# Expert weights of sparse blocks, brought to their buffers by two DMAs of the SyncE queue instead of by GpSimd

## The chip, the core and the metric

The kernel runs on one core of one Trainium2 chip. The metric is the time of one execution on the device in microseconds (us): 1469.63, the median of 3 runs (1466.67 to 1473.55). Engines are named as in the profile: PE is TensorE, PEld its weight load, ACT is ScalarE, DVE is VectorE, POOL is GpSimd, SP is SyncE. SP issues most of the DMAs here; a name with a q (SPq) is the engine's sequencer.

## The reference

Eight sequences of 512 tokens, 128 features wide, pass through five layers with residual sums:

```python
x = x + 0.5 * _L0_ffn_ref(_layernorm(x), ...)      # 8 experts, two per token   (first 8-expert stage)
x = x + _L0_attn_ref(_layernorm(x), ...)
x = x + 0.5 * _L0_ffn_ref(_layernorm(x), ...)      # the same weights again    (second 8-expert stage)
x = x + 0.5 * _L1_ffn_ref(_layernorm(x), ...)      # 16 experts
x = x + _L1_attn_ref(_layernorm(x), ...)           # a scan
x = x + 0.5 * _L1_ffn_ref(_layernorm(x), ...)
```

In an 8-expert layer a router picks two of eight experts for each token, and each expert is `gelu(x @ w1 + b1) @ w2 + b2` with a hidden width of 512:

```python
probs = jax.nn.softmax(xf @ w_router, axis=-1)
topk_w, topk_idx = jax.lax.top_k(probs, 2)
h = jax.nn.gelu(jnp.einsum('te,ieh->tih', xf, w1) + b1)
out = jnp.einsum('tih,ihe->tie', h, w2) + b2
out = jnp.sum(out * weights[..., None], axis=1)
```

## The kernel before

The change lies in the two 8-expert stages, both written by `moe0_phase` (the variable `occ` is 0 in the first and 1 in the second). A stage does not compute every expert for every token. Sequence 0 is computed densely: 8 blocks of 512 tokens, one for each expert. The tokens of the other seven sequences are sorted by expert: GpSimd writes their normalised rows to a DRAM table `xs_rows` by indirect DMAs, each expert padded to blocks of 512 rows, which makes `NBLK` = 21 sparse blocks. Which expert a block belongs to is known only at run time and stands in a small table in SBUF, `expert_t`. So a stage walks over 29 blocks: `i` = 0 to 7 dense (`D` = 8), and `i` = D + j for the sparse blocks j = 0 to 20.

All eight experts' weights lie in SBUF in `w_all`, split into a high and a low part, 4 x 512 columns for an expert: 1024 for the up product and 1024 for the down product. A dense block reads its expert's columns there, since they are fixed when the program is built. A sparse block reads copies, in `w_up[j % 2]` and `w_down[j % 2]`: two buffers each, of 128 x 1024 elements (512 KB). Before the change GpSimd makes these copies, in `take_up` (L1237) and `take_down` (L1242): it loads the expert's number into a register (L1284) and casts from a source column that the register gives (L1240, L1245). Each copy counts on the semaphore `w_taken`.

PE works a block in four chunks `c`. For each chunk it does three matmuls of the up product (`up0`, L908; matmuls at L904, L905, L906) and then three of the down product of the chunk that lies 6 chunks back (`down0`, L924). So in the step of block D + t it does up(t, 0), down(t-2, 2), up(t, 1), down(t-2, 3), up(t, 2), down(t-1, 0), four transposes back of block t-3 (`back_pe`, L974), up(t, 3), down(t-1, 1). At the start of the step stand the four transposes of the rows of the next block (`xT_pe`, L843). ACT applies gelu (L945) and makes half of the rounded copies (L950); DVE makes the other half (L958), the remainders (L960, L856) and the copy out (L990).

A buffer comes free when PE is done with it: `w_up[j % 2]` with the last up product of block j-2, at the end of the step of that block; `w_down[j % 2]` with the last down product of block j-2, which is the sixth group of the step of block j, in the middle of that step (after 12 of its 24 matmuls). `up0` and `down0` wait for `w_taken` in front of their first chunk.

The order of SP's queue in the sparse blocks is written out in `sync`: it loads block rows into three buffers `xb` (L1335, 256 KB each, up to seven ahead, held back by the wait for the transposes of the block three before), stores the result rows of each block to `ys_rows` (L1349, 256 KB, after a wait for DVE's copy), and in the first stage, behind the stores of blocks 3 to 10, saves one expert's split weights to DRAM (`keep0`, L754, 1 MB each), which the second stage reads back (L761). Every wait in this queue holds what stands behind it.

Of the kernel before, what the change touches and what calls it, by code (L numbers as in the profile page):

```python
# [7 lines left out]
F32 = mybir.dt.float32  # L8
# [9 lines left out]
NE0, HID = 8, 512  # L18
HC = HID // P
# [16 lines left out]
NBLK = (2 * (B - 1) * T + NE0 * (T - 1)) // T  # L36
# [24 lines left out]
def build(nc, a, out, phases=PHASES):  # L61
    nc.disable_value_cache = True
    with ExitStack() as ctx:
# [98 lines left out]
        w_staged = [sem(f"w_staged{i}") for i in range(4)]  # L162
# [195 lines left out]
        def load_weights(q):  # L358
# [16 lines left out]
            for dst, src in weights:  # L375
# [2 lines left out]

        moe0_sems, moe1_sems = {}, {}
        moe0_names = ("pe_step", "act_step", "dve_step", "pool_step", "dve_chain", "w_hi", "w_lo", "w_kept", "sent0", "sent1", "pads",  # L380
                      "x_ld0", "x_ld1", "x_ld2", "xT_ps", "up_ready", "act_done", "dve_done", "down_done", "yback", "w_taken")
        moe0_sems.update({k: sem(f"moe0_{k}") for k in moe0_names})
        rs_ = moe0_sems

# [294 lines left out]
        def moe0_phase(n):  # L679
# [75 lines left out]

            def reload0(e):
                if e > 3:
                    nc.sync.wait_ge(w_staged[e % 4], 32 * 3)
# [144 lines left out]
            def hi_lo(out_bank, w_hi, w_lo, x_hi, x_lo, start, stop):  # L903
                nc.tensor.matmul(out_bank, w_hi, x_hi, start=start, stop=False)  # L904
                nc.tensor.matmul(out_bank, w_hi, x_lo, start=False, stop=False)  # L905
                return nc.tensor.matmul(out_bank, w_lo, x_hi, start=False, stop=stop)  # L906

            def up0(i, c):  # L908
                u = HC * i + c
                if c == 0:  # L910
                    nc.tensor.wait_ge(s["dve_done"], dve_no("xl", prep(i)))
                    if dense(i) and occ:
                        nc.tensor.wait_ge(w_staged[i % 4], 32 * (3 + i // 4))
                    elif dense(i):
                        nc.tensor.wait_ge(s["w_lo"], i + 1)
                    else:
                        nc.tensor.wait_ge(s["w_taken"], 2 * NBLK * occ + max(1, 2 * (i - D)))
                if u > 3:
                    nc.tensor.wait_ge(s["act_done"], act_no("gelu", (u - 4) // HC, c))
                w = w_all[:, i * 4 * HID:i * 4 * HID + 2 * HID] if dense(i) else w_up[(i - D) % 2]  # L920
                q = prep(i) % 2
                hi_lo(bank[u % 4][:], w[:, c * P:(c + 1) * P], w[:, HID + c * P:HID + (c + 1) * P], xh[q][:], xl[q][:], True, True).then_inc(s["up_ready"], 1)

            def down0(i, c):  # L924
                u = HC * i + c
# [316 lines left out]
            def take_down(g, j, ex_):  # L1242
                if j > 1:
                    g.wait_ge(s["down_done"], U0 + HC * (D + j - 1))
                nc.gpsimd.tensor_copy(w_down[j % 2], w_all[:, bass.ds(ex_ * (4 * HID) + 2 * HID, 2 * HID)]).then_inc(s["w_taken"], 1)  # L1245

            def routed(g, what):

# [15 lines left out]
            def gpsimd(g):  # L1264
                after_phases(g, n)
                f = base(n + 1)
                if occ == 0:
                    route_consts(g)
                    for b in ORDER[0]:
                        seq_root(g, occ, b)  # L1270
                    group_send(g, occ, 0, pace=lambda k, m: routed(g, {4: "l4", 8: "l5", 12: "l6", 14: "l7"}.get(k)))
                    group_send(g, occ, 1, pace=lambda k, m: after_start(g, k))
                    group_send(g, occ, 2, pace=lambda k, m: beside(g, 16 + k * 15 // 16, 0))
                else:
                    seq_root(g, occ, B - 1)
# [4 lines left out]
                g.wait_ge(s["x_ld0"], 16 * (per_ld[0] * occ + 1))  # L1280
                ex_ = nc.gpsimd.value_load(expert_t[0:1, 0:1], min_val=0, max_val=NE0 - 1)
                take_up(g, 0, ex_)
                for j in range(NBLK):
                    e1 = nc.gpsimd.value_load(expert_t[0:1, j + 1:j + 2], min_val=0, max_val=NE0 - 1) if j + 1 < NBLK else None  # L1284
                    if j + 1 < NBLK:
                        take_up(g, j + 1, e1)
                    take_down(g, j, ex_)
                    ex_ = e1
                    if D + j == NORM - 3 and occ == 0:
                        g.wait_ge(w_loaded, 16 * N_WEIGHTS)  # L1290
                        for w, w_p in ((wq, wq_p), (wl, wl_p)):
                            last = g.tensor_copy(w_p[:].rearrange("p (d h) -> p d h", d=HD), w[:].rearrange("p (h d) -> p d h", d=HD))
                        last.then_inc(tables_ready, 1)
                    if D + j == NORM - 2:
                        norm_b(f)
                    for b, tile in GATHERS.get(j, ()):
                        stored_by(g, occ, b)
                        gather(g, occ, b, (tile, tile + 1))
                if occ == 0:
                    early_parts["pool"](g)  # L1300

            def sync(q_):
# [16 lines left out]
                    load_weights(q_)  # L1319
                if occ:  # L1320
                    for k in range(4):
                        q_.wait_ge(w_staged[k], 32 * 4)
# [14 lines left out]
                x_load(0)  # L1337
                q_.wait_ge(s["x_ld0"], 16 * (per_ld[0] * occ + 1))
                for i in range(1, 7):
                    x_load(i)  # L1340
                for i in range(NBLK):
                    if i + 7 < NBLK:
                        x_load(i + 7)
                    if occ == 0 and i == NBLK - 3:
                        early_parts["saves"]()
                    if occ == 0 and i == NBLK - 2:
                        early_parts["loads"]()
                    q_.wait_ge(s["dve_done"], dve_no("y", D + i))
                    q_.dma_start(rows(ys_rows, i), yb[i % 2]).then_inc(y_stored[i % 2], 16)  # L1349
                    if occ == 0 and 2 < i < 3 + NE0:  # L1350
                        keep0(i - 3)

            return {"tensor": tensor, "scalar": scalar, "vector": vector, "gpsimd": gpsimd, "sync": sync, "zeros": zeros}


# [397 lines left out]
        def attn_phase(n):  # L1753
# [195 lines left out]
            def early_act(i, c):  # L1949
                if (i, c) == (ALL - 2, 3):  # L1950
                    biased_act("q", 0, 6)
                if (i, c) == (ALL - 1, 1):
                    biased_act("k", 0, 6)
                    nc.scalar.wait_ge(moe0_sems["w_taken"], 2 * NBLK * (occ0 + 1))
                    part1_act("k", 0)

            def early_dve(v):
                v.wait_ge(moe0_sems["w_taken"], 2 * NBLK * (occ0 + 1))
                split_dve(v, "k", 0)

            def early_v_dve(v):
                v_dve(v, 0, bank[6])

            def early_pool(g):
                g.wait_ge(moe0_sems["w_taken"], 2 * NBLK * (occ0 + 1))
                split_pool(g, "q", 0)

            def early_saves():
# [1147 lines left out]
```

## Time and profile before

| | |
|---|---|
| time, median of 3 runs | 1469.63 us (1466.67 to 1473.55) |
| span of the profiled execution, first to last instruction | 1464.5 us |
| what lies around the span, by the median | 5.1 us |
| PE, DVE, ACT, POOL busy | 1277.9, 1149.4, 887.0, 520.0 us |
| sparse blocks of the first 8-expert stage | about 113 to 273 us |
| sparse blocks of the second | about 792 to 949 us |

The profiled execution has no time of its own beside its span; 1464.5 lies 2.2 us under the shortest of the three runs. In the rows below, a row of a timeline has its start, its duration, engine, line and operation, the tile written and the tiles read, and in square brackets how long the engine had sat idle before it and what released it. Buffers cut from the shared region all have the name `shared`. Lines are those of the kernel before.

### The profile page before, as it was taken

Reading aid. Unit: us, or ns where it says so; the run is one execution under the profiler, and the core shown is the slowest. Engines: PE = TensorE matmul, PEld = TensorE weight load, DVE = VectorE, ACT = ScalarE, POOL = GpSimd, SP = SyncE. Lnnn points to the kernel's source line nnn. Section 1 sums busy time; section 2 is a strip of 40 time slices with the busy share of each in tenths; the row PEclk is TensorE's granted clock in tenths of the full one; section 3 lists DMA queues with packets and bytes.
Section 4 is the critical chain, followed back from the end, with each engine's and each line's share of the span. In section 5 each row is a group of like instructions: output and inputs, shape, how many; then the busy total and the mean of one; then the engine's idle time right before and its main releaser. Section 6 shows DMA issues by size and latency. Waiting matters only on the chain.

```text
span 1464.5 us, 20418 instructions
## 1 busy us (share of the span) xinstructions
PE 1277.9 (87%) x6496; PEld 766.6 (52%) x6496; DVE 1149.4 (78%) x2430; ACT 887.0 (61%) x1402; POOL 520.0 (36%) x757
## 2 busy tenths in 40 slices
PE   6768999779999889998679999899999889899998
PEld 5557777412222222222267777666666345566665
DVE  6857879789889989889466989878886664877875
ACT  6846767348788768887577667633333477334432
POOL 6773427444534424511273335514430120210100
PEclk9989999779999989999889999999999999999999
DMA  8521453332212202210151122255453011054434
GB/s 285 143 86 52 151 196 117 129 90 86 86 45 88 86 24 91 92 35 2 66 224 56 58 73 86 78 126 114 105 118 73 13 32 24 1 127 107 92 84 116
DMA packets 88679, 133.94 MB, mean 91 GB/s; under 512 B 16756, under 2 KB 42836, under 8 KB 87548
## 3 DMA queue, kind: packets, MB, share of 16 engines
q1 hardware_dynamic: 81404, 117.93, 28.5%
q0 software_dynamic: 7168, 14.69, 3.4%
q8 instruction: 53, 0.87, 0.3%
q14 instruction: 54, 0.44, 0.1%
HBM read 82.23 MB, written 47.45 MB: 89 GB/s over the span
## 4 chain that ended last, share of the span: by engine, by line
PE 55%; DVE 25%; issue 8%; ACT 7%; DMA 3%; POOL 1%; SPq 1%; DVEq 0%; ACTq 0%; POOLq 0%
DVE shared L2170 6%; PE bank L1557 6%; PE pair L904 5%; PE pair L906 5%; PE pair L905 5%; PE bank L2248 5%; PE pair L1469 3%; PE pair L1471 3%; PE pair L1470 3%; PE pair L2230 3%; PE pair L2162 3%; DVE shared L960 3%; ACT shared L2238 2%; DVE shared L1545 1%; PE bank L974 1%
## 5 line engine op out<-in xcount | busy, mean ns | idle before, releaser
L2170 DVE TENSOR_REDUCE shared<-pair 128x2 f32<-128x1024 f32 x256 | 309.7, 1217 | 41.6 <-PE pair L2162 38.7
L2238 ACT ACTIVATE shared<-pair 128x1024 f32<-128x1024 f32 x256 | 260.5, 1022 | 51.7 <-PE pair L2230 50.2
L960 DVE TENSOR_TENSOR shared<-shared 128x512 fp32r<-128x512 f32 x232 | 193.2, 842 | 76.9 <-ACT shared L950 73.4
L904 PE MATMUL pair<-shared 128*128 128x512 f32 x464 | 198.2, 427 | 9.9 <-DMA shared<-w_keep 3.9
L1524 ACT ACTIVATE shared<-pair 128x512 f32<-128x512 f32 x144 | 85.6, 596 | 179.5 <-PE pair L1471 179.3
L906 PE MATMUL pair<-shared 128*128 128x512 f32 x464 | 187.3, 404 | 0.0
L905 PE MATMUL pair<-shared 128*128 128x512 f32 x464 | 187.3, 404 | 0.0
L945 ACT ACTIVATE shared<-pair,shared 128x512 f32<-128x512 f32 x168 | 115.9, 690 | 72.7 <-PE pair L906 67.3
L1469 PE MATMUL pair<-shared 128*128 128x512 f32 x288 | 154.4, 536 | 4.9 <-DVE shared L1479 4.9
L2248 PE MATMUL bank<-shared 128*9 128x512 f32 x1024 | 139.6, 618 | 4.5 <-ACT shared L2238 4.3
L277 POOL DMA_INDIRECT staged<-ys_rows,slots x112 | 117.7, 1051 | 58.4 <-ACT shared L2238 32.1
L645 POOL DMA_INDIRECT xs_rows<-shared,slots x112 | 118.3, 1057 | 55.5 <-issue 26.8
L1536 DVE TENSOR_TENSOR shared<-shared,pair 128x512 f32<-128x512 f32 x128 | 87.0, 682 | 58.2 <-ACT shared L1524 56.9
L1557 PE MATMUL bank<-shared,down_w 128*128 128x512 f32 x256 | 129.1, 595 | 0.8 <-DVE shared L1545 0.8
L2162 PE MATMUL pair<-shared 48*128 48x512 bf16 x512 | 104.1, 405 | 21.3 <-ACT shared L2238 10.6
L1471 PE MATMUL pair<-shared 128*128 128x512 f32 x288 | 115.5, 401 | 0.0
L1470 PE MATMUL pair<-shared 128*128 128x512 f32 x288 | 114.9, 399 | 0.0
L2230 PE MATMUL pair<-shared 51*128 51x512 bf16 x512 | 102.3, 397 | 5.9 <-DVE shared L2170 5.2
L904 PEld LDWEIGHTS pair<-shared 128*128 128x128 f32 x464 | 91.1, 196 | 28.2 <-issue 8.0
L2230 PEld LDWEIGHTS pair<-shared 51*128 51x128 bf16 x512 | 24.7, 93 | 150.9 <-issue 87.8
L906 PEld LDWEIGHTS pair<-shared 128*128 128x128 f32 x464 | 90.3, 195 | 21.5
L905 PEld LDWEIGHTS pair<-shared 128*128 128x128 f32 x464 | 90.9, 196 | 16.9 <-issue 0.2
(380 smaller groups left out, 2262.7 us busy)
## 6 DMA issues: line engine op xcount, KB each, us to landing
shared<-p_coef_rows SPq DMA_DIRECT2D x64, 512.0 KB, 6.0
shared<-xs_rows SPq DMA_DIRECT2D x42, 256.0 KB, 2.8
ys_rows<-shared SPq DMA_DIRECT2D x42, 256.0 KB, 2.0
w_keep<-shared SPq DMA_DIRECT2D x8, 1024.0 KB, 4.8
shared<-w_keep SPq DMA_DIRECT2D x16, 512.0 KB, 9.6
shared<-p_q_parts SPq DMA_DIRECT2D x64, 96.0 KB, 2.4
shared<-p_k_parts SPq DMA_DIRECT2D x64, 96.0 KB, 2.5
xs_rows<-shared SPq DMA_DIRECT2D x1, 5376.0 KB, 18.4
```

The source lines that it names most:

```text
L904: nc.tensor.matmul(out_bank, w_hi, x_hi, start=start, stop=False)
L905: nc.tensor.matmul(out_bank, w_hi, x_lo, start=False, stop=False)
L906: return nc.tensor.matmul(out_bank, w_lo, x_hi, start=False, stop=stop)
L960: nc.vector.tensor_tensor(hl[u % RING][:], hid[u % RING][:], hh[u % RING][:], ALU.subtract).then_inc(s["dve_done"], 1)
L1469: nc.tensor.matmul(out_bank, w_hi, x_hi, start=start, stop=False)
L1470: nc.tensor.matmul(out_bank, w_hi, x_lo, start=False, stop=False)
L1471: return nc.tensor.matmul(out_bank, w_lo, x_hi, start=False, stop=stop)
L1557: nc.tensor.matmul(bank[6][:], w, h, start=(j == 0), stop=(j == IT - 1)).then_inc(s["down_done"], 1)
L2170: nc.vector.tensor_reduce(mneg[:, i, 2 * c:2 * c + 2], pair_of("max", b, m)[:], AX_X, ALU.max, negate=True).then_inc(s["mx_read"], 1)
L2230: last = nc.tensor.matmul(pair_of("exp", b, 2 * st + p)[:, f, :], ka[par][rows, c, kt * P:(kt + 1) * P], qa[par][rows, c, :], start=True, ...
L2238: nc.scalar.activation(probs[st % 2][:, 2 * p:2 * p + 2, :], pair_of("exp", b, 2 * st + p)[:], ACT.Exp, scale=scale).then_inc(s["exp_done" ...
L2248: last = nc.tensor.matmul(bank[6][32 * hh:32 * hh + HD + 1, :], v_all[:, b * TILES + kt, hh % 2 * (H // 2) + g * HG // 2 + hh // 2, :], pr ...
```

## The change

GpSimd no longer copies expert weights. `take_up` and `take_down` become one DMA each, issued by SP, with a source column from a register that SP loads; the two buffers of each kind count on the four semaphores `w_staged`, which `up0` and `down0` now wait for. SP's queue is written anew: in the turn `t` of its loop stand the load of the next expert's number, the down weights of block t, the up weights of block t + 1, the rows of block t + 3, the store of block t - 4, and in the first stage a save. The wait for the first rows in front of the second load is gone. Three users of `w_all`'s space after the first stage wait for the four semaphores (`weights_taken`) instead of `w_taken`.

```diff
-                        nc.tensor.wait_ge(s["w_taken"], 2 * NBLK * occ + max(1, 2 * (i - D)))
+                        nc.tensor.wait_ge(w_staged[(i - D) % 2], taken_by(i - D))
...
-                        nc.tensor.wait_ge(s["w_taken"], 2 * NBLK * occ + min(2 * (i - D) + 3, 2 * NBLK))
+                        nc.tensor.wait_ge(w_staged[2 + (i - D) % 2], taken_by(i - D))
...
-            def take_up(g, j, ex_):
+            def take_up(q_, j, at):
                 if j > 1:
-                    g.wait_ge(s["up_ready"], U0 + HC * (D + j - 1))
-                nc.gpsimd.tensor_copy(w_up[j % 2], w_all[:, bass.ds(ex_ * (4 * HID), 2 * HID)]).then_inc(s["w_taken"], 1)
+                    q_.wait_ge(s["up_ready"], U0 + HC * (D + j - 1))
+                q_.dma_start(w_up[j % 2].bitcast(F32), w_all[:, bass.ds(at * (4 * HID), 2 * HID)].bitcast(F32)).then_inc(w_staged[j % 2], 16)
...
                 for j in range(NBLK):
-                    e1 = nc.gpsimd.value_load(expert_t[0:1, j + 1:j + 2], min_val=0, max_val=NE0 - 1) if j + 1 < NBLK else None
-                    if j + 1 < NBLK:
-                        take_up(g, j + 1, e1)
-                    take_down(g, j, ex_)
-                    ex_ = e1
+                    g.wait_ge(s["up_ready"], U0 + HC * (D + j))
...
                 x_load(0)
-                q_.wait_ge(s["x_ld0"], 16 * (per_ld[0] * occ + 1))
-                for i in range(1, 7):
-                    x_load(i)
-                for i in range(NBLK):
-                    if i + 7 < NBLK:
-                        x_load(i + 7)
...
+                of = {0: expert(0)}
+                take_up(q_, 0, of[0])
+                x_load(1)
+                x_load(2)
+                for t in range(NBLK + 4):
+                    if t + 1 < NBLK:
+                        of[t + 1] = expert(t + 1)
+                        if t == 0:
+                            take_up(q_, 1, of[1])
+                    if t < NBLK:
+                        take_down(q_, t, of.pop(t))
+                    if 0 < t and t + 1 < NBLK:
+                        take_up(q_, t + 1, of[t + 1])
+                    if t + 3 < NBLK:
+                        x_load(t + 3)
+                    if t > 3:
+                        store(t - 4)
...
+            def weights_taken(eng):
+                for k in range(4):
+                    eng.wait_ge(w_staged[k], (64 + 16 * per_st[k % 2]) * (occ0 + 1))
...
                     biased_act("k", 0, 6)
-                    nc.scalar.wait_ge(moe0_sems["w_taken"], 2 * NBLK * (occ0 + 1))
+                    weights_taken(nc.scalar)
                     part1_act("k", 0)
```

On SP, before, one turn in the middle of the first stage's sparse blocks is a load of rows, a store and a save (here two turns):

```order
L1335 DMA shared<-xs_rows 128x512 [waits moe0_xT_ps]
L1349 DMA ys_rows<-shared 128x512 [waits moe0_dve_done]
L754 DMA w_keep<-shared 128x2048
L1335 DMA shared<-xs_rows 128x512 [waits moe0_xT_ps]
L1349 DMA ys_rows<-shared 128x512 [waits moe0_dve_done]
L754 DMA w_keep<-shared 128x2048
```

On SP now, one turn at the same place; with their numbers the buffers are `shared12` = `w_all`, `shared20` and `shared21` = `w_down`, `shared3` and `shared4` = `w_up`; L1334 loads the expert's number, L1248 and L1243 are the two copies:

```order
L1334 TENSOR_LOAD shared13
L1334 ISA x2
L1248 ISA [waits moe0_down_done]
L1248 DMA shared21<-shared12 128x1024
L1243 ISA [waits moe0_up_ready]
L1243 DMA shared3<-shared12 128x1024
```

The copy of the up weights (L1243) stands behind the copy of the down weights (L1248) and behind its wait for `down_done`; behind them follow the load of rows, the store and the save as before.

On POOL, before, at the same place:

```order
L1284 TENSOR_LOAD shared
L1284 ISA x2
L1240 ISA [waits moe0_up_ready]
L1240 COPY shared<-shared 128x1024
L1245 ISA [waits moe0_down_done]
L1245 COPY shared<-shared 128x1024
```

There the copy of the up weights of block j + 1 stood ahead of that of the down weights of block j, with a wait of its own. On POOL now nothing of this is left: behind the indirect sends of the dense blocks stand at once the small copies, the norm and the gathers:

```order
L645 DMA xs_rows<-shared,slots 10752x128 [waits moe0_up_ready] x15
L1288 COPY wq_p<-w_q 128x128 [waits moe0_up_ready,w_loaded]
L1288 COPY wl_p<-w_l 128x128
L187 TENSOR_SCALAR var<-mv 128x4 [waits moe0_up_ready,mv_ready]
L189 TENSOR_TENSOR rs_y<-var,neg_half 128x4 [waits var_ready]
L277 DMA staged<-ys_rows,slots 128x128 [waits moe0_up_ready,y_stored0,y_stored1]
```

On PE, before, at the start of the step of a sparse block (the name `pair` is a pair of PSUM banks):

```order
L843 MATMUL bank<-ident,shared 128x128 [waits moe0_dve_done,moe0_x_ld0]
L843 MATMUL bank<-ident,shared 128x128 x3
L904 MATMUL pair<-shared 128x512 [waits moe0_act_done,moe0_w_taken,moe0_dve_done]
L905 MATMUL pair<-shared 128x512
L906 MATMUL pair<-shared 128x512
```

There the first up matmul waits for GpSimd's count. On PE now, the same place:

```order
L843 MATMUL bank<-ident,shared 128x128 [waits moe0_dve_done,moe0_x_ld0]
L843 MATMUL bank<-ident,shared 128x128 x3
L904 MATMUL pair<-shared 128x512 [waits moe0_act_done,w_staged0,moe0_dve_done]
L905 MATMUL pair<-shared 128x512
L906 MATMUL pair<-shared 128x512
```

No matmul has moved; the wait is now for a DMA's semaphore. The waiting L904 stands behind the transposes of the next block's rows and ahead of everything else of its step.

## Rows read from the trace of the kernel before

**Rows 1.** Timeline, PE, first stage: starts of steps 2 and 3, first matmul of step 20.

```profile
127.12 0.60 PE L843 MATMUL bank<-ident,shared 128*128 128x128 f32 x4
133.55 0.60 PE L843 MATMUL bank<-ident,shared 128*128 128x128 f32 x4
...
260.18 0.40 PE L904 MATMUL pair<-shared 128*128 128x512 f32 x1
```

**Rows 2.** Windows of 18 steps in each stage: busy us (instructions) by engine.

```profile
core 0: us, PE busy (x) PEld busy (x) DVE busy (x) ACT busy (x) POOL busy (x), PEclk, DMA share, GB/s
127.47:260.18 132.71, 122.39 (x591) 98.32 (x590) 115.27 (x184) 89.63 (x147) 59.32 (x56) 0.97 0.40 133
804.82:934.57 129.75, 119.86 (x587) 96.77 (x586) 117.28 (x198) 89.39 (x146) 57.91 (x54) 0.99 0.22 72
```

**Rows 3.** Timeline: one step of block 4 of the first stage.

```profile
143.01 0.42 DVE L958 CAST shared<-shared 128x512 fp32r<-128x512 f32 x1
...
143.65 0.47 PE L904 MATMUL pair<-shared 128*128 128x512 f32 x1
...
146.28 0.39 PE L906 MATMUL pair<-shared 128*128 128x512 f32 x1
...
146.85 1.04 POOL L1245 CAST shared<-shared 128x1024 fp32r x1 [2.52 <-PE pair L906]
...
148.64 0.69 DVE L960 TENSOR_TENSOR shared<-shared 128x512 fp32r<-128x512 f32 x1 [0.20 <-ACT shared L950]
...
149.37 1.20 POOL L1240 CAST shared<-shared 128x1024 fp32r x1 [1.47 <-PE pair L906]
...
149.70 1.41 DVE L960 TENSOR_TENSOR shared<-shared 128x512 fp32r<-128x512 f32 x1
...
150.08 0.48 PE L904 MATMUL pair<-shared 128*128 128x512 f32 x1
```

**Rows 4.** Groups by line, 113.5 to 245 us: count, busy us, mean ns.

```profile
L960 DVE TENSOR_TENSOR shared<-shared 128x512 fp32r<-128x512 f32 x72 | 66.7, 930 | 17.3 <-ACT shared L950 15.8
...
L958 DVE CAST shared<-shared 128x512 fp32r<-128x512 f32 x36 | 18.4, 511 | 0.0
```

**Rows 5.** The same, 790 to 945 us.

```profile
L960 DVE TENSOR_TENSOR shared<-shared 128x512 fp32r<-128x512 f32 x88 | 75.0, 862 | 14.6 <-ACT shared L950 13.0
...
L958 DVE CAST shared<-shared 128x512 fp32r<-128x512 f32 x42 | 24.0, 571 | 0.4 <-ACT shared L945 0.3
```

**Rows 6.** Timeline, PE: idle times in the next-to-last sparse step of each stage.

```profile
255.82 2.04 PE L1812 MATMUL bank<-xnT,wq_p 128*128 128x512 f32 x2 [3.28 <-issue]
...
932.72 0.63 PE L974 MATMUL bank<-ident,shared 128*128 128x128 f32 x4 [2.73 <-DVE shared L990]
```

**Rows 7.** DMA issues of the page: KB each, median us from issue to landing.

```profile
ys_rows<-shared SPq DMA_DIRECT2D x42, 256.0 KB, 2.0
w_keep<-shared SPq DMA_DIRECT2D x8, 1024.0 KB, 4.8
...
shared<-shared SPq DMA_DIRECT2D x72, 32.0 KB, 2.0
```

**Rows 8.** Short windows with DMA traffic (columns of rows 2).

```profile
740.00:745.00 5.00, 5.00 (x17) 3.95 (x16) 1.82 (x3) 3.27 (x7) 3.78 (x5) 0.66 1.03 418
166.80:167.30 0.50, 0.50 (x4) 0.37 (x3) 0.50 (x1) 0.50 (x2) 0.40 (x1) 1.00 1.21 459
169.30:169.80 0.50, 0.50 (x5) 0.46 (x4) 0.47 (x3) 0.15 (x1) 0.50 (x1) 1.00 1.21 262
```

**Rows 9.** Timeline: the first sparse block, and the end of the first stage.

```profile
109.95 1.11 PE L843 MATMUL bank<-ident,shared 128*128 128x128 f32 x4 [9.62 <-DMA shared<-xs_rows]
110.89 2.03 POOL L1240 CAST shared<-shared 128x1024 fp32r x2 [4.68 <-DMA shared<-xs_rows]
...
264.16 1.04 POOL L1245 CAST shared<-shared 128x1024 fp32r x1 [9.42 <-PE pair L906]
...
265.76 0.68 ACT L945 ACTIVATE shared<-pair,shared 128x512 f32<-128x512 f32 x1
```

More of the change, by code:

```diff
@@ L380, in build @@
         moe0_names = ("pe_step", "act_step", "dve_step", "pool_step", "dve_chain", "w_hi", "w_lo", "w_kept", "sent0", "sent1", "pads",
-                      "x_ld0", "x_ld1", "x_ld2", "xT_ps", "up_ready", "act_done", "dve_done", "down_done", "yback", "w_taken")
+                      "x_ld0", "x_ld1", "x_ld2", "xT_ps", "up_ready", "act_done", "dve_done", "down_done", "yback")
         moe0_sems.update({k: sem(f"moe0_{k}") for k in moe0_names})
@@ L757, in reload0 @@
                 if e > 3:
-                    nc.sync.wait_ge(w_staged[e % 4], 32 * 3)
+                    nc.sync.wait_ge(w_staged[e % 4], 32 * 3 + 16 * per_st[e % 2])
                 for k in range(2):
@@ L906, in hi_lo, with taken_by @@
                 return nc.tensor.matmul(out_bank, w_lo, x_hi, start=False, stop=stop)
+            def taken_by(j):
+                return 64 * (occ + 1) + 16 * (per_st[j % 2] * occ + j // 2 + 1)
             def up0(i, c):
@@ L912, in up0 @@
                     if dense(i) and occ:
-                        nc.tensor.wait_ge(w_staged[i % 4], 32 * (3 + i // 4))
+                        nc.tensor.wait_ge(w_staged[i % 4], 32 * (3 + i // 4) + 16 * per_st[i % 2])
                     elif dense(i):
@@ L1235, in vector, with take_down @@
                     combine(v, occ, 2)
-            def take_up(g, j, ex_):
+            def take_up(q_, j, at):
                 if j > 1:
-                    g.wait_ge(s["up_ready"], U0 + HC * (D + j - 1))
-                nc.gpsimd.tensor_copy(w_up[j % 2], w_all[:, bass.ds(ex_ * (4 * HID), 2 * HID)]).then_inc(s["w_taken"], 1)
-            def take_down(g, j, ex_):
+                    q_.wait_ge(s["up_ready"], U0 + HC * (D + j - 1))
+                q_.dma_start(w_up[j % 2].bitcast(F32), w_all[:, bass.ds(at * (4 * HID), 2 * HID)].bitcast(F32)).then_inc(w_staged[j % 2], 16)
+            def take_down(q_, j, at):
                 if j > 1:
-                    g.wait_ge(s["down_done"], U0 + HC * (D + j - 1))
-                nc.gpsimd.tensor_copy(w_down[j % 2], w_all[:, bass.ds(ex_ * (4 * HID) + 2 * HID, 2 * HID)]).then_inc(s["w_taken"], 1)
+                    q_.wait_ge(s["down_done"], U0 + HC * (D + j - 1))
+                q_.dma_start(w_down[j % 2].bitcast(F32), w_all[:, bass.ds(at * (4 * HID) + 2 * HID, 2 * HID)].bitcast(F32)).then_inc(w_staged[2 + j % 2], 16)
             def routed(g, what):
@@ L1279, in gpsimd @@
                     group_send(g, occ, 3, pace=lambda k, m: beside(g, (28 + k) * 7 // 9, 2))
-                g.wait_ge(s["x_ld0"], 16 * (per_ld[0] * occ + 1))
-                ex_ = nc.gpsimd.value_load(expert_t[0:1, 0:1], min_val=0, max_val=NE0 - 1)
-                take_up(g, 0, ex_)
                 for j in range(NBLK):
-                    e1 = nc.gpsimd.value_load(expert_t[0:1, j + 1:j + 2], min_val=0, max_val=NE0 - 1) if j + 1 < NBLK else None
-                    if j + 1 < NBLK:
-                        take_up(g, j + 1, e1)
-                    take_down(g, j, ex_)
-                    ex_ = e1
+                    g.wait_ge(s["up_ready"], U0 + HC * (D + j))
                     if D + j == NORM - 3 and occ == 0:
@@ L1321, in sync @@
                     for k in range(4):
-                        q_.wait_ge(w_staged[k], 32 * 4)
+                        q_.wait_ge(w_staged[k], 32 * 4 + 16 * per_st[k % 2])
                 else:
@@ L1335, in x_load, with expert, store @@
                     q_.dma_start(xb[i % 3], rows(xs_rows, i)).then_inc(s[f"x_ld{i % 3}"], 16)
-                x_load(0)
-                q_.wait_ge(s["x_ld0"], 16 * (per_ld[0] * occ + 1))
-                for i in range(1, 7):
-                    x_load(i)
-                for i in range(NBLK):
-                    if i + 7 < NBLK:
-                        x_load(i + 7)
+                def expert(j):
+                    return nc.sync.value_load(expert_t[0:1, j:j + 1], min_val=0, max_val=NE0 - 1)
+                def store(i):
                     if occ == 0 and i == NBLK - 3:
@@ L1351, in sync @@
                         keep0(i - 3)
+                x_load(0)
+                of = {0: expert(0)}
[15 more added lines that the diff above has]
+                        store(t - 4)
             return {"tensor": tensor, "scalar": scalar, "vector": vector, "gpsimd": gpsimd, "sync": sync, "zeros": zeros}
@@ L1953, in early_act @@
                     biased_act("k", 0, 6)
-                    nc.scalar.wait_ge(moe0_sems["w_taken"], 2 * NBLK * (occ0 + 1))
+                    weights_taken(nc.scalar)
                     part1_act("k", 0)
             def early_dve(v):
-                v.wait_ge(moe0_sems["w_taken"], 2 * NBLK * (occ0 + 1))
+                weights_taken(v)
                 split_dve(v, "k", 0)
@@ L1964, in early_pool @@
             def early_pool(g):
-                g.wait_ge(moe0_sems["w_taken"], 2 * NBLK * (occ0 + 1))
+                weights_taken(g)
                 split_pool(g, "q", 0)
```

## The prediction

> **What bounds the kernel now.** I read the page's busy times first, then windows over the two 8-expert stages, then the timeline of single steps of PE, DVE, POOL and SP, and last the DMA issues. In the sparse blocks the step is set by PE where nothing else happens: its starts lie 6.43 us apart (127.12 to 133.55) [rows 1]. From the first up matmul of block 2 to that of block 20 the 18 steps took 132.71 us in the first stage and 129.75 in the second [rows 2], 262.5 together or 7.29 a step. At 6.43 each, 36 steps would be 231.5 us, so 31.0 us are steps that something stretched. DVE is the suspect: it was busy 6.46 us a step (115.27 and 117.28 over 36) [rows 2], and PE's long idle times end at DVE's copy or on what follows it (2.73 and 3.28 us) [rows 6]. The reader should see in one step [rows 3] that DVE's remainder L960 takes 0.69 us alone and 1.41 when it overlaps POOL's copy of 149.37. The means over each stage, 930 and 862 ns for L960 and 511 and 571 for L958 [rows 4, 5], are all above the 0.69 and 0.42 of an undisturbed one [rows 3], so the copies cost DVE 72 x 0.24 + 88 x 0.17 + 36 x 0.09 + 42 x 0.15 = 41.8 us in both stages. POOL's own time matters to nobody else here.
>
> **What is removed.** 84 casts (21 blocks, two copies, two stages) of about 1.0 to 1.2 us leave POOL. On the path this is worth what DVE loses by them: 41.8 us of DVE time, 1.16 a step, leaving 5.3 a step. Against a step of 6.43 DVE then has room, and most of the 31.0 us should go. A burst of DVE work longer than the room of one step still shows, so I leave 1 us in each stage.
>
> **What is added on PE's path.** A copy by POOL was ready soon after its buffer came free: the up copy starts at the end of a step (149.37) and the next step's matmul at 150.08 does not need it, since it serves the block behind that. Now the up copy of block t + 1 stands in SP's queue behind the wait for the down products of block t - 2, which end in the middle of step t. It is needed at the first up matmul of step t + 1. This makes a loop from step to step: twelve matmuls, then the two DMAs, then the twelve matmuls of the next step, with the other twelve and the eight transposes beside the DMAs.
> - The twelve matmuls: from 143.65 to 146.28 + 0.39, 3.02 us [rows 3].
> - Waking the queue and PE: POOL began 0.18 us after that end [rows 3]; I take 0.2 for SP's wake, its register instruction and PE's start.
> - X, from the issue of the down copy to the landing of the up copy, 2 x 512 KB through one queue. No row shows a large copy from SBUF to SBUF. From below: a store of 256 KB lands in 2.0 us [rows 7], and 0.79 MB more at the fastest stretch, 459 GB/s [rows 8], add 1.7: X = 3.7. From above: a 1 MB save lands in 4.8 [rows 7], behind a store. The nearest in kind are the small copies from SBUF to SBUF, 2.0 us for 32 KB [rows 7], in which the bytes are almost nothing; with 1.05 MB at the 418 GB/s of the reload [rows 8], 2.5 us, that is 4.4 to 4.5. I take X = 4.3, nearer to that row than to the store.
>
> The loop is 3.02 + 0.2 + 4.3 = 7.52 us, over PE's 6.43 and DVE's 5.3, so it sets the step: PE waits about 1.1 us at the start of each. 36 x 7.52 = 270.7, with 2 us left over from DVE 272.7, against 262.5: **+10.2 us**. X enters 36 times; the break-even is X = 4.02.
>
> The trace gives the two copies no price as one DMA. The Trainium skill, in "DMA: Bandwidth & Descriptors", section "Anatomy of one DMA", fits 2.0 us plus the bytes at 436 GB/s; for 1.05 MB as one transfer that is an estimate of 4.4, and the sum by it would be +13.8. It is fitted there to DMAs that GpSimd issues. The same page's rules for authors say to issue a DMA early and to wait late; here the issue is late by half a step, and that is the rule that speaks against the change.
>
> **The other edits.** SP's load of the expert number has no row of its own; on POOL landing, load and start of the copy lay within 0.94 us (109.95 to 110.89) [rows 9]. On SP it runs while the queue would wait for the middle of the next step: five issues of 0.3 to 0.5 us and this load are about 3 of 7.5 us, so it costs nothing. Uncovered it would add its 0.9 to each loop. The loads of rows and the stores stand behind the copies and are wanted one and a half steps later: nothing. In eight steps of the first stage a 1 MB save stands last in the turn. 2.62 MB a turn at 418 GB/s is 6.3 us, but where the save fell to 262 GB/s [rows 8] it is 7.8, which would hold the next copies 0.3 us: I take 1 us in all, bounds 0 and 5. At the start of each stage the second load of rows no longer waits for the first (it stands behind the first copy instead); I take -0.5, bounds -2 and +1. At the end of the first stage ACT waits for all copies before it goes on to gelu (265.76); the last down copy started on POOL at 264.16 and took 1.04 [rows 9]. By DMA, 512 KB by the same reckoning takes 3.0, so ACT is about 2 us late, and PE with it: +2, bounds 0 and +3. Against that PE was slow (2.04 us for the pair of matmuls at 255.82) after its idle time [rows 6]; without the idle time I take -1.5, bounds -3 and 0. These make +1.0.
>
> **Sum.** +11 us on the span of 1464.5, that is 1475.5; with the 5.1 us by which the median lies above the span, **1480.6**.
>
> **Rivals.**
> - *The copies are quick enough, and DVE's relief wins* (faster). In the same loop X is 3.7 or less: the step is 6.9, 36 steps are 249.1 us, with 2 left over 251.1 against 262.5, and with the +1.0 of the other edits the change is -10.4: 1459. For it: the store's row, and PE's excess of 31.0 us. Against it: the 2.0 us of a copy with hardly any bytes. It decides from X below 3.8.
> - *The two effects cancel.* X near 4.0: the lost half step equals the removed stalls, within 7 us of 1470. For it: X = 4.02 lies between the two rows.
> - *The copy is slow*, because each DMA engine reads and writes SBUF at once and goes at 262 GB/s, as in the save: X = 1.9 + 4.0 = 5.9, the step 9.1, +69 with the other edits: 1538. For it only that one stretch; a DMA that both reads and writes SBUF in bulk has no row.
> - *PE's clock drops* because it idles in each step. At 3.28 us of idle time the next matmuls were slow [rows 6], but the windows with all stalls have 0.97 and 0.99 [rows 2]; a tenth of the clock over PE's 242 busy us there is 24 us. I count it within the slow side.
>
> **How the numbers follow.** About 0.5 % (7 us) is what a measurement of this kernel can tell from no change. Forecast, X from 4.2 to 5.0 (+8 to +36): 0.45. Slow copy or clock: 0.08. Cancelling (X 3.8 to 4.2): 0.26. Quick copies: 0.21. So slower 0.53, same 0.26, faster 0.21. The range leaves out most of the slow copy, and the quickest of the quick: 1459 to 1508; the forecast's own range is 1477 to 1506.
>
> **What would show it.** In the changed profile the first up matmul of most sparse steps should wait for a DMA from `shared` to `shared`, about 1 us, some 36 times; steps should be even, near 7.5 us; L960 should fall to about 0.69 and POOL by some 90 us; the long idle times before L974 should be gone. Steps at 6.4 to 6.9 without that wait would make the forecast wrong towards faster; L960 still at 0.86 or more would mean that POOL's copies were not what stretched it.

## The result, and the profile after

The changed kernel takes 1496.2 us (median of 4 runs, 1492.4 to 1502.8) against 1471.6 us for the kernel before in the same comparison (4 runs, 1466.7 to 1474.8). The ratio is 1.0191 with a 95 % interval of 1.0148 to 1.0235: slower by 25 us between the medians and by 28 us by the ratio, more than the 7 us that can be told from no change. Back matmuls are now at L977, the remainder at L963, the cast at L961, gelu at L948; L1248 and L1243 are the copies of the down and the up weights, L1331 the load of rows, L1342 the store.

The page of the changed kernel, span and busy times:

```profile
span 1497.6 us, 20444 instructions
## 1 busy us (share of the span) xinstructions
PE 1284.1 (86%) x6496; PEld 769.1 (51%) x6496; DVE 1102.7 (74%) x2430; ACT 887.1 (59%) x1402; POOL 424.9 (28%) x673
```

POOL lost 95 us and DVE 47 us, as a relief of POOL should show, and the span still grew by 33.1 us over the 1464.5 before. That is 8.5 us more than the medians differ: the profiled execution before was a quick one, and this one (1499.3 us) lies 3 us above its median. What lies around the span is here 1.7 us, so most of the 5.1 us named for the kernel before is such spread. The windows over the same 18 steps of each stage as in [rows 2], with the same columns:

```profile
128.50:274.71 146.21, 122.39 (x591) 96.68 (x589) 95.72 (x187) 90.40 (x148) 18.99 (x20) 1.00 0.69 252
817.64:961.00 143.36, 121.37 (x588) 96.23 (x586) 97.67 (x201) 89.60 (x146) 18.08 (x18) 1.00 0.56 198
```

The 36 steps took 289.57 us (8.04 each) against 262.46: +27.1 of the +33.1. PE was busy 243.76 us, 1.5 more than before, and its clock is not lower, so the new time is PE's waiting. DVE's busy time fell from 232.55 to 193.39 us. The groups by line, 113.5 to 262 us and then 803 to 973 us, answer to [rows 4, 5]:

```profile
L963 DVE TENSOR_TENSOR shared<-shared 128x512 fp32r<-128x512 f32 x73 | 50.7, 696 | 53.7 <-ACT shared L953 52.5
L961 DVE CAST shared<-shared 128x512 fp32r<-128x512 f32 x36 | 15.5, 429 | 0.0
...
L963 DVE TENSOR_TENSOR shared<-shared 128x512 fp32r<-128x512 f32 x88 | 60.6, 692 | 51.5 <-ACT shared L953 50.1
L961 DVE CAST shared<-shared 128x512 fp32r<-128x512 f32 x42 | 17.6, 420 | 0.1
```

So the copies by POOL had stretched DVE: the remainder's mean of 930 and 862 ns became 696 and 692. What replaced that is seen on PE, in the timeline of two steps of the first stage:

```profile
152.12 0.47 PE L904 MATMUL pair<-shared 128*128 128x512 f32 x1 [1.23 <-DVE shared L961]
...
154.75 0.40 PE L906 MATMUL pair<-shared 128*128 128x512 f32 x1
...
158.19 0.60 PE L843 MATMUL bank<-ident,shared 128*128 128x128 f32 x4
160.06 0.47 PE L904 MATMUL pair<-shared 128*128 128x512 f32 x1 [1.27 <-DVE shared L961]
...
168.02 0.47 PE L904 MATMUL pair<-shared 128*128 128x512 f32 x1 [1.29 <-DVE shared L963]
```

In most steps PE now idles 1.2 to 1.3 us before its first up matmul, and steps lie 7.94 us apart where nothing else happens. The rows name DVE as the releaser, but the step's time is accounted for by the two copies, and the experiments on them move it. SP's queue in the same step:

```profile
155.28 0.50 SPq L1248 DMA_DIRECT2D shared<-shared  x1
155.92 0.50 SPq L1243 DMA_DIRECT2D shared<-shared  x1
156.47 0.78 SPq L1331 DMA_DIRECT2D shared<-xs_rows  x1
157.29 1.20 SPq L1342 DMA_DIRECT2D ys_rows<-shared  x1
```

All landings of L1243 in that execution:

```profile
DMA to landing us min/median/max: 2.9/4.0/5.6
```

With the median landing, 155.92 + 4.0 = 159.92, and PE starts at 160.06. From the issue of the down copy to the landing of the up copy is 0.64 + 4.0 = 4.64 us: this is X. The loop is 3.03 us of twelve matmuls (152.12 to 155.15), 0.13 to the issue, 4.64, and 0.14 to PE's start: 7.94. (Twelve matmuls are four groups of three: the last down product of block t - 2 is the fourth group of a step, not the sixth as the description of the kernel has it.)

The rest of the +33.1 lies outside these steps. In stage 1, step 2 began 1.0 us later. From step 20 of stage 1 to its last back matmuls but one it took 19.1 us (274.71 to 293.83) against 15.6 before (260.18 to 275.77). PE at the beginning of that stretch, and then ACT in it:

```profile
274.71 0.47 PE L904 MATMUL pair<-shared 128*128 128x512 f32 x1 [2.32 <-DVE shared L993]
275.80 0.63 PE L904 MATMUL pair<-shared 128*128 128x512 f32 x1
278.00 1.05 PE L904 MATMUL pair<-shared 128*128 128x512 f32 x1
```

```profile
280.65 0.69 ACT L1888 ACTIVATE shared<-bank,vecs 128x512 f32<-128x512 f32 x1
283.46 0.62 ACT L1893 CAST shared<-shared 128x512 bf16<-128x512 f32 x1 [2.13 <-issue]
283.99 0.68 ACT L948 ACTIVATE shared<-pair,shared 128x512 f32<-128x512 f32 x1
```

The granted clock was 0.59 from 274.7 to 277.0 us and 0.75 to 280.0, behind PE's 2.32 us of idle time. ACT idles 2.13 us where its code waits for the last copies' semaphores, with a gelu that PE needs behind it. Between the stages and behind the second one the two executions differ by -5.2 and +6.7 us, nearly all of it in code that the change does not touch.

### The profile page after: what moved, and what is told of

It reads as the page before. It is cut to its first block, busy times and chain, and to the rows that moved or that the text cites. A ratio compares the mean times of both kernels' runs of the same rounds, so it can differ in the third digit from the quotient of the medians.

```text
span 1497.6 us, 20444 instructions
## 1 busy us (share of the span) xinstructions
PE 1284.1 (86%) x6496; PEld 769.1 (51%) x6496; DVE 1102.7 (74%) x2430; ACT 887.1 (59%) x1402; POOL 424.9 (28%) x673
## 4 chain that ended last, share of the span: by engine, by line
PE 52%; DVE 26%; issue 9%; ACT 7%; DMA 3%; POOL 1%; SPq 1%; DVEq 0%; ACTq 0%; POOLq 0%
PE bank L1569 6%; DVE shared L2186 6%; PE pair L904 5%; PE pair L906 4%; PE bank L2264 4%; PE pair L905 4%; DVE shared L963 4%; PE pair L1481 3%; PE pair L1483 3%; PE pair L1482 3%; PE pair L2246 3%; PE pair L2178 3%; ACT shared L2254 2%; ACT shared L953 2%; DVE shared L961 1%
## 5 line engine op out<-in xcount | busy, mean ns | idle before, releaser
L963 DVE TENSOR_TENSOR shared<-shared 128x512 fp32r<-128x512 f32 x232 | 160.5, 697 | 156.7 <-ACT shared L953 153.7
L904 PE MATMUL pair<-shared 128*128 128x512 f32 x464 | 197.8, 426 | 53.2 <-DVE shared L963 23.2
L948 ACT ACTIVATE shared<-pair,shared 128x512 f32<-128x512 f32 x168 | 115.9, 690 | 105.1 <-PE pair L906 103.3
L904 PEld LDWEIGHTS pair<-shared 128*128 128x128 f32 x464 | 90.7, 195 | 80.2 <-DVE shared L963 31.6
```

The costliest lines, as they stand in the source:

```text
L963: nc.vector.tensor_tensor(hl[u % RING][:], hid[u % RING][:], hh[u % RING][:], ALU.subtract).then_inc(s["dve_done"], 1)
```

## The experiments

**The up copy issued first.** In SP's loop the copy of the up weights of block t + 1 goes ahead of the copy of the down weights of block t, as it stood on POOL before.

```diff
-                        if t == 0:
-                            take_up(q_, 1, of[1])
+                        take_up(q_, t + 1, of[t + 1])
                     if t < NBLK:
                         take_down(q_, t, of.pop(t))
-                    if 0 < t and t + 1 < NBLK:
-                        take_up(q_, t + 1, of[t + 1])
```

> The changed kernel with one edit: in each turn of SP's loop the copy of the up weights of block t + 1 stands ahead of the copy of the down weights of block t and its wait. Loop theory (the up copy is late because it stands behind the wait for the down products, and two copies of 512 KB lie between the middle of one step and the start of the next): the wait of PE for the copy goes, the 36 steps come from 8.04 us to 6.43 to 6.7, a gain of 48 to 58 us on the changed kernel: 1440 to 1450 us, below the kernel before. Rival A (SP's queue is too full: three more entries a turn make everything late whatever the order): no gain, 1485 or more. Rival B (copies by DMA land too late or disturb the engines wherever they stand): PE still waits for them, steps over 7.3 us, 1470 or more.

Measured: 1453.3 us, ratio to the kernel before 0.9901 (0.9870 to 0.9932). It beats both kernels, though it lies 3 us above the expected 1440 to 1450. Its windows over the same steps (columns of rows 2):

```profile
129.45:254.86 125.41, 120.64 (x591) 97.48 (x590) 94.05 (x184) 89.55 (x147) 19.08 (x20) 0.99 0.79 294
794.35:916.84 122.49, 119.34 (x588) 96.91 (x586) 96.12 (x198) 89.33 (x146) 17.63 (x18) 0.99 0.66 232
```

They make 247.90, which is 41.7 less than the changed kernel and 14.6 less than the kernel before. SP's queue in two steps:

```profile
152.80 0.50 SPq L1243 DMA_DIRECT2D shared<-shared  x1
156.11 0.49 SPq L1248 DMA_DIRECT2D shared<-shared  x1
156.64 0.59 SPq L1331 DMA_DIRECT2D shared<-xs_rows  x1
157.27 0.78 SPq L1342 DMA_DIRECT2D ys_rows<-shared  x1
159.22 0.50 SPq L1243 DMA_DIRECT2D shared<-shared  x1
```

The up copy now goes out as soon as its buffer is free, at the end of a step and a whole step ahead of the matmul that needs it, and the queue turns every 6.42 us, PE's own pace. The same two DMAs with the same bytes now cost PE almost nothing: the 36 steps take 0.8 us more than without any bulk copy (next experiment). The loss lay in the order of the queue, not in DMA as the means.

**No bulk copies by POOL, in the kernel before.** From block 2 on POOL's copies take 8 columns of 1024; the rest of the weights is left out. No DMA takes their place.

```diff
-                nc.gpsimd.tensor_copy(w_up[j % 2], w_all[:, bass.ds(ex_ * (4 * HID), 2 * HID)]).then_inc(s["w_taken"], 1)
+                cut = 2 * HID if j < 2 else 8
+                nc.gpsimd.tensor_copy(w_up[j % 2][:, 0:cut], w_all[:, bass.ds(ex_ * (4 * HID), cut)]).then_inc(s["w_taken"], 1)
```

(and the same for `w_down`)

> The kernel before, in which GpSimd copies only 8 of 1024 columns from the third sparse block on (so most sparse blocks use weights of another expert; the copies' work is what is left out). It shows what the relief of DVE is worth without any DMA. Loop theory, with its term of 31.0 us of stretched steps that the copies cause through DVE: L960 falls to about 0.69 us, the 36 steps take 232 to 240 us instead of 262.5, 1441 to 1452 us. Rival C (the stretched steps come from DVE's own extra work, not from POOL's copies): steps stay above 7.0 us, 1462 us or more.

Measured: 1449.2 us, ratio 0.9880 (0.9845 to 0.9916). The windows, and the remainder's group over the whole page:

```profile
128.18:252.91 124.73, 120.36 (x591) 97.45 (x590) 93.64 (x184) 89.56 (x147) 29.81 (x55) 0.99 0.43 142
797.78:920.15 122.37, 119.20 (x587) 96.90 (x586) 95.99 (x198) 89.35 (x146) 28.50 (x53) 0.99 0.25 75
...
L960 DVE TENSOR_TENSOR shared<-shared 128x512 fp32r<-128x512 f32 x232 | 161.0, 700 | 108.3 <-ACT shared L950 105.3
```

247.10 us: the relief of DVE is worth 15.4 us of the 31.0 that lay above 6.43 a step. The time is within what was expected, but the 36 steps are not (232 to 240). DVE's instructions are at their undisturbed length (700 ns), and 15.6 us of stretched steps are still there. By the windows PE idles in 7.5 us of them (124.73 - 120.36 and 122.37 - 119.20); in the other 8.1 it is busy longer than 6.43 us a step. The longest step is step 3 of each stage, 10.63 and 10.50 us. DVE spends 4.2 us there on the sparse tokens' routing weights (133.78 to 137.99, a RECIPROCAL of 1.55 us among them), and PE's back matmuls then wait 2.4 us for `x_res`:

```profile
141.44 0.80 PE L974 MATMUL bank<-ident,shared 128*128 128x128 f32 x4 [2.41 <-DVE x_res L983]
```

Behind this wait the granted clock was 0.61 (141.4 to 143.0 us) and 0.50 (to 144.6). So DVE's own work, which was the rival here, holds a part of what is left; the rest is PE's own busy time.

**A small down copy, in the changed kernel.** From block 2 on the down copy takes 128 of its 1024 columns; the others are left out. The wait and the issue stay.

```diff
-                q_.dma_start(w_down[j % 2].bitcast(F32), w_all[:, bass.ds(at * (4 * HID) + 2 * HID, 2 * HID)].bitcast(F32)).then_inc(w_staged[2 + j % 2], 16)
+                cut = 2 * HID if j < 2 else 128
+                q_.dma_start(w_down[j % 2][:, 0:cut].bitcast(F32), w_all[:, bass.ds(at * (4 * HID) + 2 * HID, cut)].bitcast(F32)).then_inc(w_staged[2 + j % 2], 16)
```

> The changed kernel, in which the DMA of the down weights copies only 128 of 1024 columns from the third sparse block on, with the same place, wait and semaphore (down products of other experts are what is left out). Loop theory: X falls from 4.64 us to the issue of the small copy (0.64) and one copy of 512 KB (2.9), the step to 3.02 + 0.28 + 3.54 = 6.84: 36 x (8.04 - 6.84) = 43 us less, 1453 us (1445 to 1462). Rival A (SP's queue is too full): the entries are the same, no change, 1490 or more. Rival D (the time between the middle of a step and the landing is latency, not bytes): less than 10 us gained, 1486 or more.

Measured: 1471.9 us, ratio to the kernel before 1.0032 (1.0005 to 1.0058). PE's starts and SP's two issues (L1249 is the small copy):

```profile
151.22 0.47 PE L904 MATMUL pair<-shared 128*128 128x512 f32 x1 [0.53 <-DVE shared L963]
...
158.37 0.47 PE L904 MATMUL pair<-shared 128*128 128x512 f32 x1 [0.48 <-issue]
```

```profile
154.38 0.50 SPq L1249 DMA_DIRECT2D shared<-shared  x1
155.02 0.50 SPq L1243 DMA_DIRECT2D shared<-shared  x1
```

The step is 7.15 us: 448 KB less in front of the up copy saves 0.79 us a step, where a step of 6.84 and a time of 1445 to 1462 us had been expected. Over the 36 steps it is 24.9 us (264.70 in all). X is still 158.37 - 0.14 - 154.38 = 3.85. So most of X is left with hardly any bytes in front: the issue ahead, 0.64 us, and the up copy's own time from issue to landing, with a median of 3.3 us here and not the 2.9 that the expectation took.

**Another 512 KB in front of the up copy, in the changed kernel.** A DMA of 512 KB from `w_all` to DRAM is issued between the two copies, and the up products wait for it too.

```diff
+                        if i - D > 1:
+                            nc.tensor.wait_ge(s["extra"], 16 * ((NBLK - 2) * occ + i - D - 1))
...
                     q_.wait_ge(s["up_ready"], U0 + HC * (D + j - 1))
+                    q_.dma_start(extra_to[(j - 2) * P:(j - 1) * P, :], w_all[:, 0:2 * HID].bitcast(F32)).then_inc(s["extra"], 16)
                 q_.dma_start(w_up[j % 2].bitcast(F32), ...).then_inc(w_staged[j % 2], 16)
```

> The changed kernel with one more DMA of 512 KB (from SBUF to a DRAM scratch table) between the waits and the copy of the up weights, in every turn from the third block on. Loop theory: X grows by the time of its bytes, 0.52 MB at 390 to 459 GB/s, 1.15 to 1.35 us, in each of 36 steps: +41 to +49 us, 1537 to 1546. Rival A (SP's queue): only the issue counts, 0.5 us a step: +18, 1514. Rival D (latency): under +10 us.

Measured: 1577.5 us, ratio 1.0756 (1.0713 to 1.0798): +81 on the changed kernel, nearly twice what was expected. PE's starts in three steps, and windows over the two steps between them and over the 36 steps (columns of rows 2):

```profile
169.10 0.47 PE L904 MATMUL pair<-shared 128*128 128x512 f32 x1 [2.56 <-DMA shared<-shared]
...
178.23 0.47 PE L904 MATMUL pair<-shared 128*128 128x512 f32 x1 [2.46 <-DMA shared<-shared]
...
189.05 0.76 PE L904 MATMUL pair<-shared 128*128 128x512 f32 x1 [2.62 <-DVE shared L856]
```

```profile
168.50:178.00 9.50, 6.67 (x32) 5.32 (x32) 5.37 (x10) 4.94 (x8) 0.00 (x0) 1.00 0.62 229
178.00:188.60 10.60, 8.20 (x32) 6.46 (x32) 5.29 (x13) 4.95 (x8) 0.00 (x0) 0.84 0.54 196
...
127.81:314.62 186.81, 143.28 (x592) 112.26 (x590) 95.75 (x187) 90.30 (x148) 19.00 (x20) 0.87 0.66 247
854.51:1040.52 186.01, 140.31 (x588) 110.58 (x586) 99.05 (x202) 89.53 (x146) 18.07 (x18) 0.88 0.56 204
```

At full clock (1.00, the upper of two levels, 2.4 GHz) the step is 9.13, 1.2 us above 7.94, which is what was expected of the bytes. The other part is the clock: with about 2.5 us of idle PE in each step it falls in most of them (0.84 over the second of these steps, so partly at the lower level, 1.2 GHz; 0.87 and 0.88 over the two windows of 18 steps, in which PE is busy 39.8 us longer than in the changed kernel). The second step is 10.82 us, 1.69 longer than the first; 1.55 of that lie in its twelve matmuls, since SP's first issue of the turn comes 3.15 us after PE's start in the first step (172.25) and 4.70 in the second (182.93). This is the rival of the prediction in which PE's clock drops. In the changed kernel it did not come about at 1.3 us of idle time a step (clock 1.00); with twice that it did, and it nearly doubled the price. Here most rows name the DMA as releaser.

**The rows loaded ahead of the copies, in the changed kernel.** The load of rows, which ran right behind the copies, is issued one turn deeper and about 4 us ahead of them. Right behind the copies now stands the store.

```diff
                 for t in range(NBLK + 4):
+                    if t > 1 and t + 4 < NBLK:
+                        x_load(t + 4)
...
-                    if t + 3 < NBLK:
+                    if t < 2:
                         x_load(t + 3)
+                    if t == 1:
+                        x_load(5)
```

> The changed kernel, with SyncE's load of the rows of a later step issued ahead of the two weight copies of a turn (one turn deeper, so that it can go out about 3 us before them) in place of right behind them. Theory A: the row load from DRAM that runs behind the copies holds back their landing; without it the up copy lands 0.3 to 0.5 us earlier than the 4.0 us of now, the 36 steps of 7.94 us become 7.5 to 7.6, and the time falls by 11 to 18 us, to about 1480. Theory B: the up copy's landing is its own bytes, those of the down copy ahead of it and a fixed completion, and the row load has no part in it; then the landing stays at 3.9 to 4.1 us, the step at 7.9 and the time at 1496, within 4 us. Should the row load still be moving when the copies begin, the landing grows above 4.1 us and the time rises.

Measured: 1488.4 us, ratio 1.0166 (1.0123 to 1.0210). SP's queue and PE's starts:

```profile
148.48 0.33 SPq L1331 DMA_DIRECT2D shared<-xs_rows  x1
152.40 0.50 SPq L1248 DMA_DIRECT2D shared<-shared  x1
153.04 0.50 SPq L1243 DMA_DIRECT2D shared<-shared  x1
```

```profile
156.72 0.47 PE L904 MATMUL pair<-shared 128*128 128x512 f32 x1 [0.81 <-DVE shared L963]
...
164.17 0.47 PE L904 MATMUL pair<-shared 128*128 128x512 f32 x1 [0.79 <-DVE shared L961]
```

The quiet step is 7.45 to 7.47 us and the landing of L1243 has a median of 3.6 us in place of 4.0. So theory A holds for the mechanism: about 0.4 to 0.5 us of X was the row load running behind the copies. The gain over the whole kernel is smaller than the 11 to 18 us expected. The 36 steps take 280.63 us, 8.9 less, and 12 us of them lie above 7.47 each, against 4 above 7.94 in the changed kernel: in nine steps PE waits 1.1 to 2.1 us at the start and not 0.8, and why is not shown. The two ratios' intervals, each against the kernel before, overlap, and the profiled execution is the quickest of four, 11 us under their median, so the time does not show this gain; the length of the quiet steps does. Short windows over the copies show how they move:

```profile
152.90:153.40 0.50, 0.50 (x4) 0.41 (x3) 0.50 (x1) 0.41 (x1) 0.00 (x0) 1.00 0.00 0
153.40:153.90 0.50, 0.50 (x7) 0.41 (x5) 0.50 (x4) 0.50 (x2) 0.00 (x0) 1.00 0.77 311
153.90:154.40 0.50, 0.50 (x5) 0.41 (x4) 0.41 (x3) 0.50 (x2) 0.00 (x0) 1.00 1.01 401
...
155.40:155.90 0.50, 0.50 (x5) 0.27 (x3) 0.47 (x2) 0.12 (x1) 0.42 (x2) 1.00 1.02 401
```

No byte moves for 1.0 us after the issue at 152.40; then the stretch holds 401 GB/s, at which 1.05 MB take 2.6 us, to about 156.1 if the copies' bytes go ahead of the store's, and PE starts at 156.72. In the changed kernel, where the row load follows, the rate is 401 too at first and falls to 213 and 258 GB/s from 158.7 to 159.7 us, just before PE's start at 160.06.

**The up copy first, and ACT's wait later.** As the first experiment, and ACT's wait for the copies moved two chunks later, behind two more gelus of the last steps.

```diff
                 if (i, c) == (ALL - 1, 1):
                     biased_act("k", 0, 6)
+                if (i, c) == (ALL - 1, 3):
                     weights_taken(nc.scalar)
                     part1_act("k", 0)
```

> The kernel with the up copy issued first (1453.3 us, ratio to the kernel before 0.990), and besides ScalarE's wait for the next sparse stage's weights and its share of their casts moved from turn (last, 1) to turn (last, 3) of the stage. Theory: ScalarE stood 2.0 us in that wait ahead of a gelu that the last steps of stage 1 needed, so the end of stage 1 (first up matmul of step 20 to the first back matmul of the last step, 17.4 us there, 15.6 us in the kernel before) comes back to about 15.5 and the time falls by 2 us, to about 1451, ratio about 0.989. Rival: the tail is long because of the DMAs of that stretch and not of that wait; then it stays at 17 us or more and the time at 1453, and casts that come later may add up to 3 us to the start of stage 2.

Measured: 1450.6 us, ratio 0.9890 (0.9851 to 0.9929). PE's last back matmuls but one of stage 1, and ACT:

```profile
268.62 1.07 PE L977 MATMUL bank<-ident,shared 128*128 128x128 f32 x4 [2.01 <-DVE shared L993]
```

```profile
261.45 0.69 ACT L948 ACTIVATE shared<-pair,shared 128x512 f32<-128x512 f32 x1 [0.77 <-PE pair L906]
262.04 0.61 ACT L1890 CAST shared<-shared 128x512 bf16<-128x512 f32 x1
```

ACT no longer waits ahead of its cast L1890, and from the first up matmul of step 20 (254.08) to that L977 it takes 14.5 us, 2.9 less than with the up copy first alone. In the trace the wait is thus worth what the row of ACT said; in the time, 2.8 us between two medians with intervals of 4 to 6 us either way is not shown. By its median this is the fastest complete version run, 1.1 % under the kernel before, but it is not told apart from the version with the up copy first alone.

## Why the prediction was right, and where its terms were off

The time came out slower, 1496.2 us inside the range of 1459 to 1508 and inside the forecast's own 1477 to 1506, by the mechanism named: a loop from the middle of one step through SP's queue to the start of the next. The single figure, 1480.6, was 15.6 us too low. That this is so near to the error of the loop's term alone (15.1, below) is chance: the profiled spans differ by 33.1 us, and the sum for them was 11.

- *What is removed.* Right in kind: DVE's remainder fell to 0.69 us, POOL by 95 us, DVE's busy time in the 36 steps by 39.2 us (41.8 over both stages was the forecast). Wrong in worth: "most of the 31.0 us should go" did not hold. Without the bulk copies 15.4 us went. The windows of rows 2 already showed that this was too much: PE was busy in 242.25 of the 262.46 us, so only 20.2 of the 31.0 were idle time. Nor did rows 6 bear the whole reading put on them: the wait of 3.28 us names no engine that released it, and both rows are of the end of a stage. In the changed kernel this did not matter, since the loop set the step; in the rival in which DVE's relief wins, the 2 us left over would have been too few.
- *The loop.* Shown, by taking it apart: with the up copy issued before the wait for the down products, the time goes from 1.019 to 0.990 of the kernel before. Of its terms, the 3.02 us of matmuls stood (3.03); the two wakes were 0.27 and not 0.2; X was 4.64 and not 4.3. The step is then 7.94 in place of 7.52, and 36 x 0.42 = 15.1 us is the largest error of the sum.
- *X.* The reckoning took the fixed part of a copy with hardly any bytes and added all bytes at 418 GB/s. The bytes moved at 401. What it left out is the row load behind the copies, which held them back by 0.4 to 0.5 us. With the load ahead of them and the store behind, X is 156.72 - 0.14 - 152.40 = 4.18. The prediction had said of loads and stores behind the copies that they cost nothing, because it asked only when their own data was wanted. The Trainium skill's fit in "DMA: Bandwidth & Descriptors", section "Anatomy of one DMA", gave an estimate of 4.4 us for X, between the value chosen and the measured one. For one copy of 512 KB it gives an estimate of 3.2, where the landings here begin at 2.9.
- *What is late next.* 2 us were left for stretched steps and 1 for the saves, 3.7 came in all (289.57 - 36 x 7.94).
- *The other edits.* Without the saves 0 was forecast, and +4.5 came at the two ends of stage 1. ACT's wait was right at 2.1 us (forecast 2, shown by moving it). At the start neither the -0.5 nor the +1.0 can be told from the spread between executions: the transposes of the second step began at 120.67 us before, at 121.72 after, and between 119.51 and 122.65 in the six experiments. And the 1.5 us that a missing slow stretch should have given back did not come: PE idles 2.32 us before step 20 and is slow behind it, with 0.63 and 1.05 us for L904.
- *Rivals.* The quick copies would have needed X below 3.8, and even with 128 columns of the down copy it is 3.85. The slow copy at 262 GB/s is refuted by 401; the save's row of 262 had a row load behind it as well, issued at 167.02, and was no row of one transfer alone. The clock did not fall at 1.3 us of idle time a step, but the run with 2.5 shows that this rival was near.

The advice to issue a DMA early and to wait late, in the Trainium skill's "DMA: Bandwidth & Descriptors", section "Rules for kernel authors", which the prediction set against the change, is what the first experiment follows; the traces here agree with it, at 41.7 us over the 36 steps.

Left open: why the stretch between the stages was 5.2 us shorter and that behind the second 6.7 us longer in the changed execution. No run was made on it; they nearly cancel. Left open too is why, with the rows loaded earlier, so many steps are longer than their loop.

## What to carry to other kernels

When copies move from an engine with its own waits into one in-order queue, write the entries in the order in which their buffers come free, and not in the order in which the data belongs together; one entry behind a later wait turned a gain of 15 us over these steps into a loss of 27. Price a transfer with what the queue issues right behind it, not only with what stands ahead. And when a stall is put down to one cause, take from its excess first what the engine was busy in and what other causes leave, before the rest is booked as a gain.

## What the runs showed of the hardware

- A copy of 512 KB from SBUF to SBUF landed 2.9 us after its issue at best (medians from 3.0 to 4.7 by what stood around it); one of 64 KB had a median of 1.8 us. Two of 512 KB in a row, with a store behind them, moved at 401 GB/s, after 1.0 us in which no byte moved.
- A releaser named in a row can be the wrong one of several: in the steps above, PE's rows named DVE although the wait followed the copies in every experiment on them; the order in time of SP's issue, the landing and PE's start tells it.
- PE's granted clock stood at 1.00 with 1.3 us of idle time at the start of every step of 7.94 us, and had a mean of 0.87 and 0.88 when it was about 2.5 us in steps of 8.8 to 11.7 us. The slower matmuls then lengthen the loop by which PE waits, so the cost of a longer wait nearly doubled: 2.3 us a step for a DMA whose bytes cost 1.2. A single wait did not always do the same: behind one of 3.13 us in the kernel before (to 141.45) the clock stayed at 1.00, behind one of 2.41 us without the bulk copies it was 0.61 and then 0.50.
